# Two heads side by side in the TensorE array for the rough scores, one set of shift products, new engine orders and a stepped routing

## The chip, the cores and the metric

The kernel runs on one core of one Trainium2 chip. The metric is the device time of one execution in microseconds (us), the median of several runs. TensorE (PE) multiplies a loaded 128-column matrix with a moving one; VectorE (DVE), ScalarE (ACT) and GpSimd (POOL) work on 128 partitions; SyncE (SP) issues DMA transfers. Matrix products land in eight PSUM banks, everything else lives in SBUF.

## The reference

The input x is 8 sequences of 512 tokens with 128 features. The output is x plus attention times a gate:

```python
xn = _layernorm(x, axis=-1)
s = _L0_attn_ref(xn, W_qkv, W_out)        # 32 query heads of 64, 16 key/value heads, causal, ALiBi bias
g = _silu(_L0_ffn_ref(xn, gate_w, gate_b, w1, b1, w2, b2))   # 8 experts of width 512, top 2, softmax weights
x = x + s * g
```

Scores are q times k over sqrt(64), plus slope times (key position minus query position), with keys behind the query only; softmax; times v; all heads concatenated and projected. The feed-forward part picks two experts for each token and adds their weighted outputs.

## The kernel before, in words

Attention is cut into 64 bodies: one body is one sequence and one pair of key/value heads. A body has two slots (one key/value head each, `sl`), and a slot has two query heads (`h`). Every f32 value goes through TensorE as two f16 halves (hi and lo) in three products, to keep f32 precision.

The first 32 bodies (`HALF`) are followed by the expert part (blocks of 256 gathered token rows, loops over `hidden` and `down`), then come the other 32 bodies. During the first 32 bodies GpSimd also scatters the token rows to the slots of their experts (tasks `I` and `D`, two indirect DMAs for each 128 tokens), and the expert weights are split (`W`). During the second 32 GpSimd gathers the expert outputs (`I`, `D`, `G`).

The work of a body is cut into tasks with one letter and a number:

- `Q0`, `Q1`, `K0`, `V0`: projections of queries, keys, values (PE, then ACT takes the hi half and DVE the lo half; SP stacks copies of q and k into `q_st` and `k_st` by DMA).
- `M`, `B`: the rough scores. The f16 hi halves of q and k are multiplied (`M`, function `rough`, into the banks `M_ps[0]` for the first head and `M_ps[1]` for the second), and DVE takes each query row's maximum with the mask and bias (`B`, function `peaks`). A head has three rounds: one product of 512 columns, two of 128 and 384, one of 256. So a body has 12 `M` tasks and 12 `B` tasks. The array's rows are the 128 rows of `q_raw`, which hold both heads; `k_st` has two extra planes (2 and 3) in which the keys stand in one half and zeros in the other, so that one product sees one head only.
- `C`: the maxima become the shift that softmax subtracts. They stand in columns of `spread`; four products with the identity turn them into rows (PE, function `turn_shifts`, into `M_ps[0]`), and ACT copies a row for each head into `q_st` (function `shifts`). Two `C` tasks a body, one a slot.
- `S`, `E`, `L`, `P`: exact scores in ten groups a body (PE), exponentials (ACT), the lo half of the exponentials (POOL, `t_lo`), products with the values (PE, 12 products of 64 or 65 columns a group).
- `N`, `A`, `O0`: normalise (DVE), hi and lo of the output (ACT, DVE), a transposing DMA (SP), projection with W_out (PE) and accumulation (DVE).

The order of the tasks on each engine is a table, `ORDER`: for each half and engine a list of (task, body offset, place). `one_window` issues the list once for each window `w`, a task with offset `o` for body `w + o`. An engine works its list strictly in this order and waits at semaphores. `G_USERS` says which tasks share the two PSUM banks `G_ps`, and `bank_free` waits for the user before. `run_bodies` writes the first and last windows out and puts the rest in a loop of two windows. The top-2 routing (which slot each token goes to) is computed on DVE: `choose` in three steps among the first `B` tasks, and the rest in one piece between the entry windows and window 0. PE's rank products stand there too. Products of window 0 wait for `routed`, since the ranks lie in a PSUM bank that they need.

## Time and profile before

| what | value |
|---|---|
| median of 3 runs | 1255.06 us (1253.67 to 1255.94) |
| the profiled execution | 1253.06 us |
| its span, first to last instruction | 1251.1 us |
| busy share of PE, DVE, ACT, POOL | 92%, 80%, 75%, 70% |
| mean granted TensorE clock | 0.981 of full |

A share is busy time over the span. PE counts as busy while any product is in flight, and products overlap, so a busy PE can still have room between the starts of its products. A row of a timeline gives the start, the duration and the instruction, and in brackets the idle time before it and what ended it.

### The profile page before, as it was taken

What the parts mean: (1) busy time and instruction counts of PE and PEld (TensorE: products, weight loads), DVE (VectorE), ACT (ScalarE), POOL (GpSimd) and SP (SyncE); (2) the same over time, 40 slices, a digit from 0 to 9 for tenths busy, and PEclk for the clock granted to TensorE, in tenths of its full rate; (3) what the DMA queues carried; (4) which work ended last, traced back from release to release, by engine and by line L of the source; (5) the groups of instructions that cost most, each with busy time, mean ns of one, the idle gap of its engine ahead of it and who ended that gap; (6) DMA issues with size and microseconds to landing.
All of it is one profiled execution on the core that took longest, in us unless ns stands there. A gap on an engine that the chain in (4) does not pass through costs nothing. (4 is left out here: it accounts for less than half of the span.)

```text
span 1251.1 us, 52908 instructions
## 1 busy us (share of the span) xinstructions
PE 1154.0 (92%) x17226; PEld 912.5 (73%) x17226; DVE 1005.5 (80%) x3099; ACT 939.0 (75%) x1807; POOL 878.3 (70%) x1086
## 2 busy tenths in 40 slices
PE   2579999999999999987999779999999999999994
PEld 0357777777777777766888657777777777777873
DVE  8778888888888888764777648888888888888885
ACT  2468888888888888775666458888888888888884
POOL 9048888888888888875000058888888888888885
PEclk9989999999999999999999979999999999999997
DMA  8326666666666666644433456555555555555663
GB/s 243 158 57 144 143 147 151 143 143 144 144 144 144 144 143 143 147 107 86 87 90 86 94 129 141 136 135 134 134 134 134 134 134 134 134 134 134 138 139 95
DMA packets 286161, 165.28 MB, mean 132 GB/s; under 512 B 174994, under 2 KB 274674, under 8 KB 285428
## 3 DMA queue, kind: packets, MB, share of 16 engines
q1 hardware_dynamic: 281972, 155.63, 54.7%
q0 software_dynamic: 4096, 8.40, 2.3%
q8 instruction: 59, 0.97, 0.3%
q14 instruction: 34, 0.28, 0.1%
HBM read 15.76 MB, written 16.78 MB: 26 GB/s over the span
## 5 line engine op out<-in xcount | busy, mean ns | idle before, releaser
L781 POOL TENSOR_TENSOR t_lo<-stage 128x512 f16<-128x512 f32 x640 | 654.4, 1038 | 148.7 <-ACT stage L1180 144.5
L1392 DVE CUSTOM_DVE_ANT_0 stage<-ps,kmask 128x512 bf16<-128x512 f32 (+3 forms) x1024 | 466.2, 488 | 110.7 <-PE ps L878 91.9
L1180 ACT ACTIVATE stage<-ps,slope 128x512 f32<-128x512 f32 (+1 forms) x768 | 456.8, 620 | 126.8 <-PE ps L913 80.7
L904 PE MATMUL ps<-q_st,k_st 128*128 128x256 f16 (+3 forms) x1024 | 302.5, 301 | 4.0 <-DMA k_st<-stage 1.8
L936 PE MATMUL outs<-v_sp,stage 128*128 128x65 f16 x2560 | 283.3, 194 | 12.2 <-DVE stage L1422 9.0
L938 PE MATMUL outs<-v_sp,stage 128*128 128x64 f16 x2560 | 283.1, 194 | 0.0
L940 PE MATMUL outs<-v_sp,t_lo 128*128 128x65 f16 x2560 | 283.0, 194 | 0.0
L878 PE MATMUL ps<-k_st,stage 128*128 128x512 f16 (+3 forms) x1024 | 252.8, 304 | 14.9 <-DVE spread L1392 7.6
L936 PEld LDWEIGHTS outs<-v_sp,stage 128*128 128x128 bf16 x2560 | 239.4, 98 | 21.5 <-issue 11.2
L938 PEld LDWEIGHTS outs<-v_sp,stage 128*128 128x128 bf16 x2560 | 236.5, 98 | 8.9 <-issue 0.3
L940 PEld LDWEIGHTS outs<-v_sp,t_lo 128*128 128x128 f16 x2560 | 236.5, 98 | 0.0
L905 PE MATMUL ps<-q_st,k_st 128*128 128x128 f16 x1024 | 224.0, 219 | 0.0
L908 PE MATMUL ps<-q_st,k_st 67*128 67x384 f16 (+2 forms) x768 | 211.5, 275 | 0.0
L1169 ACT CAST q_st<-ps 1x512 f16<-1x512 f32 x256 | 147.9, 578 | 32.5 <-PE ps L887 27.2
L913 PE MATMUL ps<-late_q,late_k 66*128 66x134 f16 (+1 forms) x640 | 136.0, 212 | 0.0
L904 PEld LDWEIGHTS ps<-q_st,k_st 128*128 128x128 f16 x1024 | 100.4, 98 | 34.7 <-issue 14.3
L734 POOL COPY slot_now<-slot_of 128x1 uint32 (+1 forms) x128 | 23.2, 183 | 144.6 <-DMA slot_y<-stage 144.6
L878 PEld LDWEIGHTS ps<-k_st,stage 128*128 128x128 f16 x1024 | 84.3, 98 | 53.0 <-issue 24.3
L1125 ACT ACTIVATE stage<-ps,qscale 128x512 f16<-128x512 f32 x128 | 88.5, 691 | 44.9 <-PE ps L816 36.9
L905 PEld LDWEIGHTS ps<-q_st,k_st 128*128 128x128 f16 x1024 | 100.4, 98 | 17.2 <-issue 0.6
L908 PEld LDWEIGHTS ps<-q_st,k_st 67*128 67x128 f16 x768 | 74.8, 97 | 51.7 <-issue 1.9
L1422 DVE TENSOR_TENSOR stage<-outs,stage 128x512 f16<-128x512 f32 x128 | 88.0, 687 | 21.7 <-ACT stage L1160 21.7
(205 smaller groups left out, 2702.1 us busy)
## 6 DMA issues: line engine op xcount, KB each, us to landing
k_st<-stage SPq DMA_DIRECT2D x256, 128.0 KB, 2.4
q_st<-stage SPq DMA_DIRECT2D x256, 128.0 KB, 2.4
q_st<-stage SPq DMA_DIRECT2D x256, 64.0 KB, 2.1
k_st<-stage SPq DMA_DIRECT2D x128, 64.0 KB, 2.1
slot_y<-stage SPq DMA_DIRECT2D x40, 128.0 KB, 2.0
X<-in_L_attn_inputs SPq DMA_DIRECT2D x8, 512.0 KB, 8.0
slot_x<-att SPq DMA_DIRECT2D x2, 2048.0 KB, 8.7
wx_raw<-in_L_ffn_w SPq DMA_DIRECT2D x64, 64.0 KB
```

The source lines that it names most:

```text
L781: pool.tensor_tensor(t_lo[r], t_p[r], upper(t_p[r]), ALU.subtract).then_inc(s[f"lo{u % NG}"], 1)
L878: mm = pe.matmul(M_ps[h][:, c0:c0 + w], q_raw[sl][:, 0, i * P:(i + 1) * P], k_st[par][sl][:, 2 + h, 0:w], start=True, stop=True)
L904: pe.matmul(d, k[:, 0, at], q[:, 0, seen], start=(c0 == 0), stop=False, skip_group_check=True)
L905: pe.matmul(d[:, 0:P], k[:, 1, at], q[:, 1, at], start=False, stop=True, skip_group_check=True)
L908: pe.matmul(d[:, P:], k[far, 1, at], q[far, 1, (kt + 1) * P:SEQ], start=False, stop=True, skip_group_check=True)
L913: pe.matmul(d, late_k[late, :], late_q[late, LATE:P].unsqueeze(1).to_broadcast([P - LATE - 1, len(first), P - LATE]), start=False, stop=Tr ...
L936: pe.matmul(d, p_hi, v[:, with_one], start=(opens and i == kt), stop=False, skip_group_check=True)
L938: pe.matmul(d[:, OUT_COL[sl]:OUT_COL[sl] + DH], p_hi, v[:, lo], start=False, stop=False, skip_group_check=True)
L940: mm = pe.matmul(d, t_lo[r][:, c], v[:, with_one], start=False, stop=(closes and i == QT - 1), skip_group_check=True)
L1169: ins = act.copy(q_st[sl][h][DH:DH + 1, 1, :], M_ps[0][SHIFT[h]:SHIFT[h] + 1, :])
L1180: e = act.activation(t_p[r][:, c0:c1], S_ps[u % 2][:, c0:c1], ACT.Exp, scale=slope[:, bass.ds(pair_index(n) * 2 * SLOTS + sl * 2 + h, 1)])
L1392: ins = dve.tensor_tensor_reduce(junk[h][:, c0:c0 + w], M_ps[h][:, c0:c0 + w], kmask[:, SEQ - w:SEQ], -1.0 / 1024, 3e38, ALU.add, ALU.min, ...
```

## The change

1. Rough scores. `rough` now takes both heads of a round in one `M` task: for each piece of columns one product on the array's rows 0 to 63 (head 0, into `M_ps[0]`) and one on rows 64 to 127 (head 1, into `M_ps[1]`). Six `M` tasks a body in place of twelve; the number and width of the products stays. A round now waits for the peaks of both heads of the round before. The zero-padded planes of `k_st` are gone, and with them one of three DMAs of each key stacking and half of another.
2. Shifts. One `C0` on PE for both slots: the four head maxima stand in columns 0, 32, 64, 96 of one `spread` buffer (two buffers, by body parity), four products in place of eight, into a bank of `G_ps` and no longer into `M_ps[0]`. ACT still copies four rows.
3. All of `ORDER` and `G_USERS` are new.
4. Routing. The piece ahead of window 0 is cut into eight steps `route(0..7)`, put behind tasks of windows 0 to 2 of DVE (`FIRST_ONES`); PE's ranks stand behind a `V0`, and ACT copies them out of PSUM (`kept`). Scattering starts at body 4 in place of body 2; in bodies 7, 10, 13 and 16 two groups of 128 tokens are sent, with a third buffer.
5. Small: the first `V` task behind the `Q` tasks, the Exp table loaded earlier, windows 0 to 17 of the first half written out, ACT's last fill task of the second half ahead of the last expert output.

```diff
@@ rough scores and shifts on PE
-                sl, r, h = round_of(j)
+                sl, r = divmod(j, NR)
                 need(pe, f"qh{sl}", n + 1)
-                need(pe, f"kst{sl}", (n + 1) * 48)
-                if r > 0:
-                    need(pe, f"peak{sl}{h}", n * NR + r)
-                elif h == 0:
-                    need(pe, f"crow{1 - sl}", n + sl)
-                else:
-                    need(pe, f"peak{1 - sl}{h}", (n + sl) * NR)
+                need(pe, f"kst{sl}", (n + 1) * 32)
+                for h in range(2):
+                    if r > 0:
+                        need(pe, f"peak{sl}{h}", n * NR + r)
+                    else:
+                        need(pe, f"peak{1 - sl}{h}", (n + sl) * NR)
...
                 for i, c0 in ROUNDS[r]:
                     w = (i + 1) * P
-                    mm = pe.matmul(M_ps[h][:, c0:c0 + w], q_raw[sl][:, 0, i * P:(i + 1) * P],
-                                   k_st[par][sl][:, 2 + h, 0:w], start=True, stop=True)
-                mm.then_inc(s[f"rough{sl}{h}"], 1)
-
-            def turn_shifts(n, _, sl):
-
-                for h in range(2):
-                    need(pe, f"peak{sl}{h}", (n + 1) * NR)
-                for i in range(QT):
-                    mm = pe.matmul(M_ps[0][:, i * P:(i + 1) * P], spread[sl][:, i, :], ident16[:, :],
-                                   start=True, stop=True)
-                mm.then_inc(s[f"turnc{sl}"], 1)
+                    for h in range(2):
+                        head = slice(DH * h, DH * h + DH)
+                        mm = pe.matmul(M_ps[h][:, c0:c0 + w], q_raw[sl][head, 0, i * P:(i + 1) * P],
+                                       k_st[par][sl][head, 0, 0:w], start=True, stop=True)
+                mm.then_inc(s[f"rough{sl}"], 1)
+
+            def turn_shifts(n, par, _):
+
+                bank_free(n, "C0")
+                for sl in range(SLOTS):
+                    for h in range(2):
+                        need(pe, f"peak{sl}{h}", (n + 1) * NR)
+                for i in range(QT):
+                    mm = pe.matmul(bank_of("C0")[:, i * P:(i + 1) * P], spread[par][:, i, :], ident16[:, :],
+                                   start=True, stop=True)
+                mm.then_inc(s["turnc"], 1)
@@ key stacking on SP
-                sp.dma_start(to[DH:2 * DH, 0:4:3, :], hi.unsqueeze(1).to_broadcast([DH, 2, SEQ]))\
-                  .then_inc(s[f"kst{sl}"], 16)
-                sp.dma_start(to[0:DH, 2, :], hi).then_inc(s[f"kst{sl}"], 16)
+                sp.dma_start(to[DH:2 * DH, 0, :], hi).then_inc(s[f"kst{sl}"], 16)
@@ peaks on DVE
-                dve.wait_ge(s[f"rough{sl}{h}"], n * NR + r + 1)
+                dve.wait_ge(s[f"rough{sl}"], n * NR + r + 1)
@@ the sharing of the two G banks
-        [("V0", 1), ("O0", -2)],
-        [("Q1", 1), ("K0", 2), ("Q0", 2)],
+        [("Q1", 1), ("K0", 2), ("O0", -2)],
+        [("V0", 1), ("Q0", 2), ("C0", 1)],
@@ the first lines of PE's order of the first half
-            ("S0", 0, 0), ("M11", 0, 2), ("S1", 0, 3), ("P7", -1, 6), ("C1", 0, 9), ("P8", -1, 10), ("P9", -1, 13),
+            ("S0", 0, 0), ("M1", 1, 3), ("P9", -1, 5), ("S1", 0, 7), ("S2", 0, 11), ("Q1", 1, 14), ("M2", 1, 19),
@@ which groups of 128 tokens are sent with body n
+        FIRST_SENT, TWICE = 4, (7, 10, 13, 16)
-            return [t for t in range(NT) if min(t + UNROLL, HALF - UNROLL + (t - NT) // 2 + UNROLL) == n]
+            t = n - FIRST_SENT + len([b for b in TWICE if b <= n])
+            more = [(t - 1, UNROLL, TWICE.index(n))] if n in TWICE else []
+            return more + [(t, n % UNROLL, (n - FIRST_SENT) // UNROLL)]
@@ where the routing steps stand
-        CHOICE = {"B1": 0, "B3": 1, "B5": 2}
+        FIRST_ONES = {"DVE": [("B1", 0), ("B3", 0), ("B5", 0), ("B3", 1), ("B5", 1), ("N0", 0), ("B3", 2), ("B5", 2),
+                              ("N0", 1), ("B3", 3), ("B5", 3)],
+                      "PE": [("V0", 1)], "ACT": [("E4", 0)]}
```

Before the change, PE in its loop of the first half has the two heads' rounds of 256 columns (L878) apart, with a group of exact scores (L904 to L913) between them; L936 and L938 are products with the values.

```order
L878 MATMUL ps<-k_st,stage 128x256
L904 MATMUL ps<-q_st,k_st 128x512
L905 MATMUL ps<-q_st,k_st 128x128
L908 MATMUL ps<-q_st,k_st 128x384
L913 MATMUL ps<-late_q,late_k 128x67
L878 MATMUL ps<-k_st,stage 128x256
L936 MATMUL outs<-v_sp,stage 128x65
L938 MATMUL outs<-v_sp,stage 128x64
```

In the changed program the same round in the loop (L891 is `rough`, L825 to L827 are the three products of a projection) is:

```order
L825 MATMUL ps<-xT_hi,wq_hi 128x512
L826 REGISTER_ALU
L826 MATMUL ps<-xT_lo,wq_hi 128x512
L827 REGISTER_ALU
L827 MATMUL ps<-xT_hi,wq_lo 128x512
L301 REGISTER_ALU
L891 MATMUL ps<-k_st,stage 128x256 x2
```

The two heads' products now stand next to each other and nothing is between them; a round is between a query projection and a value projection.

On DVE before the change, the peaks (L1392) of two rounds follow each other with no other task between, here the loop's rounds of 128 and 384 columns of the second head and then the round of 256; L1400 is the lo half of the queries.

```order
L1392 ISA stage,spread<-ps,kmask 128x128
L1392 ISA spread 128x1
L1392 ISA stage,spread<-ps,kmask 128x384
L1392 ISA spread 128x1
L1385 REGISTER_ALU
L1392 ISA stage,spread<-ps,kmask 128x256
L1392 ISA spread 128x1
L1392 ISA stage,spread<-ps,kmask 128x256
L1392 ISA spread 128x1
L1400 ISA
```

In the changed program the normalisation (L1498, L1501) stands between these two rounds (L1462 is `peaks`, L1470 the lo half of the queries).

```order
L1462 ISA spread 128x1
L301 ISA
L1498 RECIPROCAL rden<-outs 128x8
L1501 TENSOR_TENSOR outs<-outs,rden 128x2x4x64
L1455 REGISTER_ALU
L1462 ISA stage,spread<-ps,kmask 128x256
L1462 ISA spread 128x1
L1462 ISA stage,spread<-ps,kmask 128x256
L1462 ISA spread 128x1
```

After the change each round's peaks are parted from the next round's by one or more other DVE tasks.

At the start, DVE of the changed program has the routing between tasks of windows 0 to 2. This is the place of `route(2)` in window 0 (L1419 to L1422), with the normalisation ahead of it and the peaks of a later round behind it:

```order
L1501 TENSOR_TENSOR outs<-outs,rden 128x2x4x64
L1419 TENSOR_TENSOR wx_lo<-per_e,ecmp 128x64
L1420 TENSOR_REDUCE per_e<-wx_lo 128x8
L1421 TENSOR_TENSOR per_e<-per_e 128x8
L1422 TENSOR_SCALAR per_e<-per_e 128x8
L1462 ISA stage,spread<-ps,kmask 128x256
L1462 ISA spread 128x1
```

Before, these four stood with 23 others in one run ahead of window 0 (L1478 to L1519), of which these are the first rows:

```order
L1478 TENSOR_SCALAR top<-top 128x32
L1479 RECIPROCAL top<-top 128x32
L1480 TENSOR_TENSOR top<-top 128x32
L1483 TENSOR_SCALAR ecmp<-ecmp 128x64
L1487 TENSOR_TENSOR wx_lo<-outs,wx_lo 128x128
L1489 TENSOR_REDUCE per_e<-wx_lo 128x8
```

The run is gone from between the peaks and window 0, and its rows are spread over three windows.

## Rows read from the trace of the kernel before

**Rows 1.** The page: busy shares, and tenths in 40 slices of 31.3 us.

```profile
PE 1154.0 (92%) x17226; PEld 912.5 (73%) x17226; DVE 1005.5 (80%) x3099; ACT 939.0 (75%) x1807; POOL 878.3 (70%) x1086
PE   2579999999999999987999779999999999999994
```

**Rows 2.** Windows, all engines: busy us of each, clock, DMA share, GB/s.

```profile
67.50:76.20 8.70, 0.07 (x2) 0.00 (x0) 8.05 (x25) 0.85 (x2) 2.04 (x2) 0.79 0.00 0
250.00:500.00 250.00, 248.54 (x3906) 198.48 (x3905) 216.95 (x693) 209.08 (x403) 216.81 (x259) 1.00 0.63 143
1000.00:1200.00 200.00, 199.75 (x3110) 158.24 (x3108) 170.75 (x550) 166.32 (x309) 163.41 (x194) 1.00 0.60 135
```

**Rows 3.** One instruction a body, in each half: durations ns, first and last start.

```profile
L1140 ACT ACTIVATE v_sp<-ps x25: 597/632/635, 127.9 to 500.6; 128x512 f16<-128x512 f32 x25
L1140 ACT ACTIVATE v_sp<-ps x25: 616/617/621, 809.8 to 1185.1; 128x512 f16<-128x512 f32 x25
```

**Rows 4.** Timeline of PE, first half: start us, duration us, instruction.

```profile
301.38 0.38 PE L887 MATMUL ps<-ident,spread 128*128 128x128 f16 x4
301.60 0.19 PE L936 MATMUL outs<-v_sp,stage 128*128 128x65 f16 x1
...
301.96 0.38 PE L814 MATMUL ps<-xT_hi,wk_hi 128*128 x1
...
302.61 0.27 PE L904 MATMUL ps<-q_st,k_st 128*128 128x256 f16 x1
302.72 0.22 PE L905 MATMUL ps<-q_st,k_st 128*128 128x128 f16 x1
...
303.60 0.59 PE L878 MATMUL ps<-k_st,stage 128*128 128x512 f16 x2
304.03 0.22 PE L814 MATMUL ps<-wo_hi,aT 128*128 x1
...
305.37 0.33 PE L904 MATMUL ps<-q_st,k_st 128*128 128x384 f16 x1
305.53 0.22 PE L905 MATMUL ps<-q_st,k_st 128*128 128x128 f16 x1
```

**Rows 5.** Groups by line and form, 250 to 500 us: busy us, mean ns, idle before.

```profile
L1392 DVE CUSTOM_DVE_ANT_0 stage<-ps,kmask 128x512 bf16<-128x512 f32 x66 | 42.8, 686 | 8.3 <-PE ps L878 8.3
L1392 DVE CUSTOM_DVE_ANT_0 stage<-ps,kmask 128x256 bf16<-128x256 f32 x64 | 27.2, 425 | 9.0 <-PE ps L878 4.0
L1407 DVE SCALAR_TENSOR_TENSOR stage<-ps,stage 128x512 f16<-128x512 f32 x16 | 11.1, 692 | 11.7 <-ACT stage L1133 11.7
L1180 ACT ACTIVATE stage<-ps,slope 128x512 f32<-128x512 f32 x129 | 88.8, 700 | 34.8 <-PE ps L913 34.8
L781 POOL TENSOR_TENSOR t_lo<-stage 128x512 f16<-128x512 f32 x162 | 166.5, 1036 | 27.9 <-ACT stage L1180 26.3
L758 POOL DMA_INDIRECT slot_x<-row_now,slot_now x32 | 31.9, 997 | 5.1 <-issue 5.1
L746 POOL TENSOR_TENSOR row_now<-mix,row_now 128x128 f16<-128x128 f16 x16 | 7.0, 436 | 0.5
L734 POOL COPY slot_now<-slot_of 128x1 uint32 x33 | 6.1, 185 | 0.0
```

**Rows 6.** Timeline of DVE and then PE at the start.

```profile
64.83 0.18 DVE L1478 TENSOR_SCALAR top<-top 128x32 f32<-128x32 f32 x1 [0.94 <-ACT top L1233]
...
75.14 0.23 DVE L1519 TENSOR_TENSOR slot_of<-slot_of,slot_bits 128x64 uint32<-128x64 uint32 x1
...
76.28 0.59 PE L887 MATMUL ps<-ident,spread 128*128 128x128 f16 x4 [8.71 <-DVE spread L1392]
```

**Rows 7.** Timeline of SP's queue, first half.

```profile
304.67 0.63 SPq L550 DMA_DIRECT2D k_st<-stage  x1
305.35 0.59 SPq L552 DMA_DIRECT2D k_st<-stage  x1
305.99 0.59 SPq L553 DMA_DIRECT2D k_st<-stage  x1
306.81 0.62 SPq L538 DMA_DIRECT2D q_st<-stage  x1
```

More of the change, by code:

```diff
@@ L289, in build @@
                 s[f"{step}{u}"] = sem(f"s_{step}{u}")
-        for step in ("rough", "peak"):
-            for j in ("00", "01", "10", "11"):
-                s[f"{step}{j}"] = sem(f"s_{step}{j}")
+        for sl in range(SLOTS):
+            s[f"rough{sl}"] = sem(f"s_rough{sl}")
+            for h in range(2):
+                s[f"peak{sl}{h}"] = sem(f"s_peak{sl}{h}")
         block = ctx.enter_context(nc.Block())
@@ L344, in run_bodies @@
         def run_bodies(eng, engine_name, tasks, lo, hi):
-            start, end = lo + 2 * UNROLL, hi - 2 * UNROLL
+            start, end = lo + (max(TWICE) + UNROLL if lo == 0 else 2 * UNROLL), hi - UNROLL
             for w in range(lo, start):
@@ L420, in weights_split, with over_e @@
             eng.wait_ge(s["wlo"], len(SPLITS))
+        L, t1, one1, L2, one2, cw = (lg[:, i, :, :] for i in range(6))
+        rank_of, total_of = L, t1[:, 0, :]
+        def over_e(a):
+            return a.unsqueeze(2).to_broadcast([P, NT, E])
+        ev = eidx[:, :].unsqueeze(1).to_broadcast([P, NT, E])
         RANK = E * FC
@@ L694, in _ @@
                     pool.memset(v_sp[par][:, :, col:col + 1], 1.0)
-            for sl in range(SLOTS):
-                pool.memset(spread[sl][:, :, :], 0.0)
+            for par in range(UNROLL):
+                pool.memset(spread[par][:, :, :], 0.0)
             for i in range(WORD):
@@ L1080, in _ @@
                         step_of(i_, c, g)
-            for j in ("00", "01", "10", "11"):
-                pe.wait_ge(s[f"peak{j}"], HALF * NR)
+            for sl in range(SLOTS):
+                for h in range(2):
+                    pe.wait_ge(s[f"peak{sl}{h}"], HALF * NR)
             for sl in range(SLOTS):
@@ L1288, in _ @@
                     outputs(j, c - 1)
+            begin_half("ACT", tasks, HALF, BODIES, fill_part(STEPS - 1, STEP - 1, 0))
             outputs(STEPS - 1, STEP - 1)
-            for g in range(PARTS):
+            for g in range(1, PARTS):
                 begin_half("ACT", tasks, HALF, BODIES, fill_part(STEPS - 1, STEP - 1, g))
@@ L1474, in _ @@
             dve.wait_ge(s["attz"], 1)
-            enter_bodies("DVE", {**tasks, "Y": lambda n, _, k: choose(k)}, 0, HALF)
-            dve.wait_ge(s["topexp"], 1)
-            small(dve.tensor_scalar(top[:, 6, :], top[:, 5, :], WS, WS, ALU.mult, ALU.add))
-            small(dve.reciprocal(top[:, 6, :], top[:, 6, :]))
-            small(dve.tensor_tensor(top[:, 7, :], top[:, 6, :], top[:, 5, :], ALU.mult))
-            blocks, first, end, first_slot = (per_e[:, i, :] for i in range(4))
-            small(dve.tensor_scalar(ecmp[:, :, :], ecmp[:, :, :], 0.0, None, ALU.is_gt))
@@ L1523, in _ @@
             dve.wait_ge(s["zeros"], 16 * ZERO_DMAS)
-            run_bodies(dve, "DVE", tasks, 0, HALF)
+            run_bodies(dve, "DVE", {**tasks, "Y": lambda k: route(k - CHOICES)}, 0, HALF)
             leave_bodies("DVE", tasks, 0, HALF, late=LATE_O)
```

218 lines of the change are left out of this document (117 added, 101 removed), and 48 rows, old and new, of the table ORDER.

## The prediction

> **What bounds the kernel now.** I read the page first. PE is busy 92% of the span, and in the tenths by slices it is at 9 but at the start, at two places in the middle (into the expert part and out of it) and at the end [rows 1]. So I cut out stretches of the two attention halves. From 250 to 500 us PE is busy 248.5 of 250 us, at full clock, DVE and POOL 217 and ACT 209; from 1000 to 1200 us PE has 199.75 of 200, DVE 171, ACT 166 and POOL 163 [rows 2]. TensorE is the bound, but a busy share can't say by how much, since products overlap. I take the time of a body from an instruction that runs once in each: 24 intervals from 127.9 to 500.6 us are 15.53 us a body, and 24 from 809.8 to 1185.1 are 15.64 [rows 3].
>
> For PE's real floor I use start to start. Four products of 128 columns take 0.22 us (301.38 to 301.60), so 0.056 each. Twelve with the values take 0.36, so 0.030 each. Three of 512 take 0.65 (301.96 to 302.61), so 0.216 each; 256 columns take 0.11 and 384 take 0.16 [rows 4]. A body has 120 value products (3.60 us), exact scores (a head takes 0.54 for L904's widths of 512, 384, 256 and 128, 0.33 for L908's 384, 256 and 128, 0.22 for four of L905, so four heads 4.36), ten late marks of 67 or 134 columns (0.48), rough scores 4 x (0.216 + 0.16 + 0.11 + 0.056) = 2.17, projections of queries, keys and values 1.30 + 0.65 + 0.67, output projection 24 x 0.056 = 1.34, shifts 8 x 0.056 = 0.45. The sum is 15.0 us. The kernel needs 15.53 and 15.64, so it runs 3.5 to 4% above the floor of its busiest engine. The waits agree: ACT sits 34.8 us of these 250 until PE's scores, POOL 27.9 until ACT, DVE 8.3 and 4.0 until PE's rough scores and 11.7 until ACT [rows 5].
>
> The floors of the others follow from the shares: DVE 216.95/250 x 15.53 = 13.5, POOL 13.5 and another 0.3 of issue time ahead of its two indirect DMAs (5.1 us for 32), ACT 13.0 [rows 2, 5]. In the second half, 13.35, 12.8 and 13.0.
>
> **The change, part by part.** *Rough scores.* The same 16 products of 2.17 us a body, but now in pairs on separate halves of the array's rows and into separate banks. No product of this trace uses 64 rows, so the price of a pair has to be bounded. If a pair runs one behind the other, it costs what it costs now: 0 saved. If the two stream together, half goes: 1.08 us a body. I take the second, since nothing in the two products is shared (rows, operands' partitions, bank) and issue is no obstacle: value products with their weight loads start every 0.030 us [rows 4], so the second of a pair of 512 could start 0.03 behind the first. With that lag a body's eight pairs give back 0.2, and I keep 0.9 to 1.1 saved.
>
> The trace has only one kind of array use, so what it costs to go from 128 rows to 64 and back is unknown too. From below it is nothing. From above it is a full drain: a product of 128 columns lasts 0.22 us where the next starts after 0.056, so 0.16 us [rows 4], 12 times a body (six rounds, in and out), 1.9 us. I take near nothing, because the nearest thing in the rows, the step from one kind of product to another (L887 to L936 at 301.60, L878 to L814 at 304.03), shows no gap at all; the drain is a rival below.
>
> The Trainium skill bears on both. Its page "TensorE: Matmul & The Clock Gate", Part 3, says that products on distinct row groups run at once with starts some 4 ns apart. By that page the pairs would save the whole 1.08. Its page "TensorEngine Tiling (Array Packing)", Key Properties, says that changing the tiling mode drains TensorE. By that rule there would be twelve drains a body and, at the price above, the rival's time below. No run so far shows either.
>
> *Shifts.* Four products fewer a body, 0.22 us of PE. ACT's four row copies stay. The old `turn_shifts` used `M_ps[0]`, so rough scores waited for ACT's copies; now they wait for the peaks alone.
>
> *Floor after.* 15.0 - 1.0 - 0.22 = 13.7 to 13.8 us on PE. That is level with POOL's 13.8 in the first half and close to DVE's 13.5. Nothing is taken off these two. So the body falls not by 1.3 but to the common floor and what four nearly full engines lose to each other. One full engine lost 3.5 to 4%; for three I take 5%: 13.75 x 1.05 = 14.45 us. The best I can argue is the old 3%, 14.2; the worst 15.0, where the gain of PE is half lost.
>
> *Order.* A round now waits for both heads' peaks, so the two banks no longer take turns. In the old order the peaks of one round followed those of the next at once; in the new one DVE always has another task of 0.5 to 1.4 us between, in which PE can refill both banks (the excerpts of the order show it). What queues behind a late round on PE is a projection or a value group, and behind late peaks on DVE the normalisation that ACT and the transposing DMA wait for. I cost it inside the 5%.
>
> *SP.* Each key stacking was three DMAs of 0.63 to 0.68 us on the queue (304.67 to 306.81 with the gap) [rows 7]; one goes, twice a body, 1.3 us of queue time. PE's steady stretch shows no wait of note for keys (its idle time is 1.5 of 250 us [rows 2]), so this is worth nothing by itself. The DMA engines are at 0.63 [rows 2].
>
> *Number of bodies.* The full-rate stretch of the first half is from about 88 to 540 us, 452/15.53 = 29 bodies; of the second from 740 to 1215, 475/15.64 = 30. The saving is 29 x 1.08 + 30 x 1.19 = 67 us.
>
> *Sending.* The first sends come two bodies later, and four bodies send twice: another two indirect DMAs (2 x 1.0 and 2 x 0.16), one subtraction (0.44) and two copies (0.37) on POOL, 3.1 us [rows 5]. Against 14.45 a POOL with 13.8 + 3.1 overruns by 2.4; buffers of exponentials take up part, and the old kernel doubled up in two bodies too. Net cost 4 us (0 to 8).
>
> *Routing.* DVE's run from 64.83 to 75.37 us holds PE up for 8.7 us [rows 6], and in 67.50 to 76.20 PE does nothing [rows 2]. Spread over windows 0 to 2 it adds 3.5 us to each; with no accumulation yet (0.69) DVE needs 13.5 - 0.7 + 3.5 = 16.3 there against 14.45, so 5.6 us come back. Net gain 3 us (0 to 8). The rest (tables loaded earlier, fill order, the transition to the second half) I put at 0, plus or minus 4.
>
> *Sum.* The profiled execution had 1253.06 us: 1253 - 67 + 4 - 3 = 1187. Runs have their median 2 us above it, 1255.06, so 1189.
>
> **The rivals.**
> - *The pairs don't overlap.* For: nothing in this trace shows that two products ever do more than pipeline. Then PE's floor is 15.0 - 0.22 = 14.8, times 1.035 is 15.3; 29 x 0.23 + 30 x 0.34 = 17 us less, with the +1 of the other parts 1239 us. The change would then not do what it says.
> - *A drain at each change of rows.* For: six rounds a body, each wedged between products on all rows. Against: no such gap between different products today. With 0.16 us, 12 times, PE's floor is 13.75 + 1.9 = 15.65, times 1.035 is 16.2: 29 x 0.67 + 30 x 0.56 = 36 us more, 1292 us: slower. It decides from (15.0 - 13.75)/12 = 0.10 us a switch on.
> - *The rounds in lockstep.* Both heads wait for each other. If each of six rounds makes DVE idle 0.25 us (it idled 0.13 for each of 64 rounds of 512 columns before [rows 5]), DVE's 13.5 becomes 15.0: 29 x 0.53 + 30 x 0.64 = 35 less, 1221 us. For: DVE is nearly full. Against: the tasks that the order puts between.
>
> **How the numbers follow.** Chances: the forecast 0.64 (own range 1174 to 1208, from 14.2 to 14.75 us a body), no overlap 0.13, drain 0.13, lockstep 0.10. A measurement of this kernel tells 0.2% (2.5 us) from no change. Faster are the forecast, lockstep, most of no overlap, and a drain below 0.1 us: 0.83. Same 0.03, slower 0.14. The range leaves out 1 in 10 or so above (a dear drain) and a little below: 1172 to 1245.
>
> **What the profile after would show.** The two products of a pair of 512 start within 0.05 us of each other, not 0.216, and the round lasts some 0.25 us from its start to the next product's. The once-a-body ACT instruction comes every 14.2 to 14.8 us. DVE and POOL are busy 93% or more of a steady stretch, and idle times on DVE shift from waiting for L878's successor to waits of all kinds. PE has no idle time of 8 us near 70 us. Four windows of the first half are longer by 1 to 2 us. I am wrong if pairs start 0.2 us apart, if a gap of 0.1 us or more stands ahead of or behind each round, or if bodies take over 15 us with PE's floor at 13.8.

## The result, and the profile after

The changed kernel takes 1240.49 us (median of 4 runs, 1236.63 to 1241.53) against 1254.37 us of the kernel before, measured beside it: ratio 0.9884, 95% interval 0.9861 to 0.9907. It is 1.2% faster where 5.2% was forecast (1189 us), still inside the stated range of 1172 to 1245. The profiled execution's span is 1238.8 us, 12.3 less than before.

The busy shares of the changed kernel, as in [rows 1], and the weight loads (PEld) of its rough products.

```profile
PE 1134.3 (92%) x16970; PEld 836.3 (68%) x16970; DVE 994.9 (80%) x3099; ACT 929.2 (75%) x1808; POOL 873.8 (71%) x1082
L891 PEld LDWEIGHTS ps<-k_st,stage 64*128 64x128 f16 x1024 | 40.1, 93 | 109.9 <-issue 95.1
```

PE stays at 92%. The second row is a first clue: the 1024 loads of 64 rows have 109.9 us of idle time ahead of them, 95.1 of it "issue", that is, a wait for nothing the profile can name. Some of that is normal: the same loads on all rows have 53.1 us of it (the run e1 below, `issue: 53.1, 111`). The 42 us on top are about 0.11 for each of the 384 visits (64 bodies of six rounds).

Windows of the changed kernel, columns as in [rows 2]:

```profile
75.00:100.00 25.00, 19.37 (x262) 13.40 (x262) 19.41 (x62) 14.14 (x27) 11.32 (x12) 0.86 0.37 74
100.00:125.00 25.00, 20.96 (x299) 15.02 (x297) 20.77 (x69) 17.43 (x35) 15.14 (x15) 0.93 0.46 94
250.00:500.00 250.00, 246.30 (x3846) 178.49 (x3844) 212.24 (x689) 207.97 (x404) 220.27 (x268) 1.00 0.58 129
```

In the steady stretch PE is still busy 246.3 of 250 us. DVE is at 85% (87% before) and POOL at 88% (87% before). So four nearly full engines, which the forecast had, never came about. The third number from the end is the granted TensorE clock: 0.86 and 0.93 in the first two stretches, so a part of each ran at the lower of the clock's two levels, 1.2 in place of 2.4 GHz. The two missing shares add up to at most 5 us (0.14 x 25 + 0.07 x 25, an estimate).

The instruction that runs once a body, as in [rows 3]; the first row is the first windows, the second the steady part of the first half, the third that of the second half:

```profile
L1158 ACT ACTIVATE v_sp<-ps x5: 597/597/599, 132.6 to 193.0; 128x512 f16<-128x512 f32 x5
L1158 ACT ACTIVATE v_sp<-ps x16: 596/597/600, 258.2 to 491.9; 128x512 f16<-128x512 f32 x16
L1158 ACT ACTIVATE v_sp<-ps x26: 610/612/622, 796.5 to 1181.2; 128x512 f16<-128x512 f32 x26
```

That is 15.10, 15.58 and 15.39 us a body, against 15.53 and 15.64 before; forecast was 14.45.

The timeline of PE in the first half, to be read against [rows 4]:

```profile
302.26 0.38 PE L827 MATMUL ps<-xT_hi,wq_lo 128*128 128x512 f16 x1
302.57 0.28 PE L891 MATMUL ps<-k_st,stage 64*128 64x256 f16 x2
302.78 0.23 PE L825 MATMUL ps<-wv_hi,xT_hi 128*128 128x128 f16 x1
...
304.38 0.22 PE L928 MATMUL ps<-late_q,late_k 66*128 66x134 f16 x1
304.54 0.39 PE L891 MATMUL ps<-k_st,stage 64*128 64x512 f16 x2
304.86 0.39 PE L825 MATMUL ps<-xT_hi,wk_hi 128*128 128x512 f16 x1
...
305.30 0.38 PE L827 MATMUL ps<-xT_hi,wk_lo 128*128 128x512 f16 x1
```

The pair overlaps as forecast: two products of 512 columns are one row of 0.39 us, 0.01 longer than one alone (L827), where two on all rows took 0.59 [rows 4]. But a gap stands on either side. The product at 304.38 has 134 columns, worth 0.06, so the pair could start at 304.44 and starts at 304.54: 0.10. A product of 512 needs 0.216 until the next start, which would be 304.76; L825 starts at 304.86: 0.10 again. From 304.44 to 304.86 is 0.42 to 0.43 us, exactly what the two products took on full rows (303.60 to 304.03 in [rows 4]). For 256 columns it is worse: from 302.48 (302.26 plus 0.216) to 302.78 is 0.30, where two on full rows need 0.22. A gap of 0.1 us on either side of each round was one of the prediction's own signs of being wrong.

The weight loads around the same pair change their place too:

```profile
304.53 0.10 PEld L891 LDWEIGHTS ps<-k_st,stage 64*128 64x128 f16 x2
304.85 0.10 PEld L825 LDWEIGHTS ps<-xT_hi,wk_hi 128*128 128x128 f16 x1 [0.23 <-issue]
305.09 0.10 PEld L827 LDWEIGHTS ps<-xT_hi,wk_lo 128*128 128x128 f16 x1
```

L827's load (305.09) runs beneath the product before it and is 0.21 us ahead of its own (305.30). L891's and L825's loads are not pulled ahead: each begins 0.01 us before its product. So at a change between 64 and 128 rows no load runs ahead. Whether the 0.10 us are the load itself, which lasts as long, or the array running empty, these rows can't tell.

**Where 12.3 us of span came from.** The same instruction, before and after, between like bodies:

```profile
L1140 ACT ACTIVATE v_sp<-ps x4: 597/598/634, 81.6 to 127.9; 128x512 f16<-128x512 f32 x4
L1140 ACT ACTIVATE v_sp<-ps x26: 597/632/635, 127.9 to 515.9; 128x512 f16<-128x512 f32 x26
L1140 ACT ACTIVATE v_sp<-ps x3: 628/630/632, 515.9 to 555.8; 128x512 f16<-128x512 f32 x3
L1140 ACT ACTIVATE v_sp<-ps x30: 606/617/621, 762.8 to 1215.8; 128x512 f16<-128x512 f32 x30
```

```profile
L1158 ACT ACTIVATE v_sp<-ps x4: 597/603/629, 73.9 to 132.6; 128x512 f16<-128x512 f32 x4
L1158 ACT ACTIVATE v_sp<-ps x26: 590/597/600, 132.6 to 522.7; 128x512 f16<-128x512 f32 x26
L1158 ACT ACTIVATE v_sp<-ps x3: 597/597/597, 522.7 to 553.1; 128x512 f16<-128x512 f32 x3
L1158 ACT ACTIVATE v_sp<-ps x30: 610/612/622, 751.4 to 1196.5; 128x512 f16<-128x512 f32 x30
```

The start got worse: the first body is 7.7 us earlier (73.9 against 81.6, the routing run is gone), but three windows then take 58.7 us in place of 46.3, so window 3 begins 4.7 us later. The next 25 bodies take 390.1 us in place of 388.0, and 8 us of that are the doubled sends: without them (the run e9 below, `132.1 to 514.4`) the same 25 take 382.3, 0.23 less a body than before. The last two of the half take 30.4 us in place of 39.9, 9.5 saved. There the kernel before had its own doubled sends (bodies 30 and 31), and its PE stood for 6.2 us behind DVE (`PE outs L936 <- DVE stage L1422: 6.2, 2, 4.2`), DVE behind ACT (`DVE stage L1422 <- ACT stage L1160: 7.3, 2, 4.8`), and ACT behind the DMA of a send (`ACT row_now L1204 <- DMA slot_x<-row_now,slot_now: 7.6, 3, 4.2`). In the second half 29 bodies take 445.1 us in place of 453.0, 0.27 less each. The rest, 1.7 us, lies in the expert part and the ends.

So a steady body became 0.23 to 0.27 us shorter. The prediction's price for the four shift products that are gone is 0.22 us a body. That fits, but no run here takes the shifts out, so what shortens the steady bodies is not shown; the third key DMA, below, is another candidate for a part.

### The profile page after: what moved, and what is told of

Same layout as the page of the kernel before. It is cut to its first block and busy times, and to the rows that moved or that the text cites. A ratio compares the mean times of both kernels' runs of the same rounds, so it can differ in the third digit from the quotient of the medians.

```text
span 1238.8 us, 51239 instructions
## 1 busy us (share of the span) xinstructions
PE 1134.3 (92%) x16970; PEld 836.3 (68%) x16970; DVE 994.9 (80%) x3099; ACT 929.2 (75%) x1808; POOL 873.8 (71%) x1082
## 5 line engine op out<-in xcount | busy, mean ns | idle before, releaser
L1462 DVE CUSTOM_DVE_ANT_0 stage<-ps,kmask 128x512 bf16<-128x512 f32 (+3 forms) x1024 | 451.5, 488 | 109.4 <-PE ps L891 84.3
L1198 ACT ACTIVATE stage<-ps,slope 128x512 f32<-128x512 f32 (+1 forms) x768 | 440.7, 618 | 96.5 <-PE ps L928 83.9
L951 PE MATMUL outs<-v_sp,stage 128*128 128x65 f16 x2560 | 263.4, 195 | 6.8 <-POOL t_lo L792 5.9
L953 PE MATMUL outs<-v_sp,stage 128*128 128x64 f16 x2560 | 262.3, 194 | 0.0
L955 PE MATMUL outs<-v_sp,t_lo 128*128 128x65 f16 x2560 | 262.2, 194 | 0.0
L891 PE MATMUL ps<-k_st,stage 64*128 64x512 f16 (+3 forms) x1024 | 139.0, 309 | 25.0 <-DVE spread L1462 23.5
L747 POOL COPY slot_now<-slot_of 128x1 uint32 (+1 forms) x128 | 23.1, 183 | 153.2 <-DMA slot_y<-stage 153.2
L891 PEld LDWEIGHTS ps<-k_st,stage 64*128 64x128 f16 x1024 | 40.1, 93 | 109.9 <-issue 95.1
L1281 ACT ACTIVATE X<-ps,b1T 128x256 f32<-128x256 f32 x160 | 67.1, 472 | 57.1 <-PE ps L827 57.1
```

Source lines behind the costliest of these rows:

```text
L891: mm = pe.matmul(M_ps[h][:, c0:c0 + w], q_raw[sl][head, 0, i * P:(i + 1) * P], k_st[par][sl][head, 0, 0:w], start=True, stop=True)
L951: pe.matmul(d, p_hi, v[:, with_one], start=(opens and i == kt), stop=False, skip_group_check=True)
L953: pe.matmul(d[:, OUT_COL[sl]:OUT_COL[sl] + DH], p_hi, v[:, lo], start=False, stop=False, skip_group_check=True)
L955: mm = pe.matmul(d, t_lo[r][:, c], v[:, with_one], start=False, stop=(closes and i == QT - 1), skip_group_check=True)
L1198: e = act.activation(t_p[r][:, c0:c1], S_ps[u % 2][:, c0:c1], ACT.Exp, scale=slope[:, bass.ds(pair_index(n) * 2 * SLOTS + sl * 2 + h, 1)])
L1462: ins = dve.tensor_tensor_reduce(junk[h][:, c0:c0 + w], M_ps[h][:, c0:c0 + w], kmask[:, SEQ - w:SEQ], -1.0 / 1024, 3e38, ALU.add, ALU.min, ...
```

## The experiments

Edits are against the changed kernel unless said; ratios are to the kernel before, measured beside each run. "After" below is the changed kernel's 0.9884 [0.9861, 0.9907].

**Pairs against full rows: e1_full_rows and e2_half_columns.** In e1 each rough product runs on all 128 rows, so it adds both heads' scores, and the slopes are 0 to keep exponentials small. TensorE streams what it did before the change, with no change of rows. e2 is e1 with half the columns of each rough product (half of the rough scores are left out): the streaming time of the pairs without their switches.

```diff
-                        mm = pe.matmul(M_ps[h][:, c0:c0 + w], q_raw[sl][head, 0, i * P:(i + 1) * P],
-                                       k_st[par][sl][head, 0, 0:w], start=True, stop=True)
+                        mm = pe.matmul(M_ps[h][:, c0:c0 + w], q_raw[sl][:, 0, i * P:(i + 1) * P],
+                                       k_st[par][sl][:, 0, 0:w], start=True, stop=True)
```

> The changed kernel with one thing undone: each rough product runs on all 128 rows of the array again (it then adds up both heads, so the shifts are wrong; all ALiBi slopes are set to 0 so that exponentials stay finite; nothing of that changes the amount of work). Theory A, a switch between 128 and 64 rows costs 0.1 us each and eats what the pairs save: 12 x 0.1 = 1.2 us of switches go and 8 x 0.135 = 1.08 us of streaming come back, so the time stays within 5 us of the changed kernel's 1240. Rival B, the pairs save 1.08 us a body and something else bounds the body at 15.4 us: PE then has 1.08 us more a body, and the time rises by 20 to 60 us.

> As the run before (all 128 rows, slopes 0), but each rough product has only half its columns, so half of the rough scores is left out: PE streams exactly what the pairs stream, and there is no switch of rows. Theory A: the body falls to what I forecast for the changed kernel, 14.3 to 14.7 us, and the time to 1185 to 1205. Rival B (DVE, POOL, ACT or the waits between them hold the body at 15.4 us, whatever PE does): 1230 to 1245.

e1: 0.9867 [0.9843, 0.9891], no slower than the pairs. e2: 0.9539 [0.9519, 0.9559]. The once-a-body instruction of e1 (first windows, second half):

```profile
L1157 ACT ACTIVATE v_sp<-ps x4: 597/597/597, 136.7 to 181.5; 128x512 f16<-128x512 f32 x4
L1157 ACT ACTIVATE v_sp<-ps x26: 586/605/622, 802.9 to 1187.1; 128x512 f16<-128x512 f32 x26
```

and of e2 (first windows, steady first half, second half):

```profile
L1157 ACT ACTIVATE v_sp<-ps x4: 599/640/643, 135.0 to 177.9; 128x512 f16<-128x512 f32 x4
L1157 ACT ACTIVATE v_sp<-ps x17: 597/640/643, 254.1 to 493.1; 128x512 f16<-128x512 f32 x17
L1157 ACT ACTIVATE v_sp<-ps x27: 584/620/631, 765.1 to 1146.7; 128x512 f16<-128x512 f32 x27
```

e1 needs 14.93 and 15.37 us a body, the pairs 15.10 and 15.39: on the whole, side by side in the array saves TensorE nothing. e2 needs 14.30, 14.94 and 14.68, where 14.45 was forecast. So the other engines would have allowed most of the forecast: e2's ratio is 0.0345 below the changed kernel's, 43 us of 1254. That is what the switches cost this kernel. On TensorE alone they are 71 us (12 x 0.10 in 59 bodies); without them the bodies run into other waits, so not all of it comes back.

**The price of a switch by itself: e3_micro, e5_micro_lines.** Both are a short run of products on data in SBUF and compute nothing of the reference. In e3 one line issued everything and the trace merged the rows, so it could not tell the kinds apart; e5 gives each kind a line of its own.

> PE alone on constants, nothing waits: runs of twelve products of 512 columns on 128 rows, on rows 0 to 63 only, on rows 0 to 63 and 64 to 127 in turn into separate banks, then rounds of six 128-column products on 128 rows followed by a pair on halves of 512 or of 128 columns, the same pair on all 128 rows, and on 67 rows. Theory A: halves in turn start 0.11 us apart on average (two in 0.216), and each pair on halves among products on 128 rows has some 0.1 us of gap ahead of it and behind it, 0.2 a round, whatever its width; 67 rows show no gap. Rival B: no gap beyond 0.02 us without the kernel's waits.

> The isolated TensorE test again, each kind of product on a line of its own so that the trace keeps them apart. After the first test, theory A: twelve products of 512 columns take 2.59 us on 128 rows and on 64 rows of one half, and 1.3 us on halves in turn; a pair of 512 among 128-row products takes 0.32 us from its start to the next product's start and starts 0.1 us late (0.43 together, as two products on 128 rows take, so a round of 512 gains nothing), a pair of 128 costs 0.27 together against 0.11 on 128 rows, so it loses 0.15; with 67 rows there is no gap. Rival: gaps of 0.1 us only in the full kernel.

e5 on PE. L47 is twelve full-row products of 512 columns as a mark, L55 twelve in turn on the upper and lower half, L51 twelve on rows 0 to 63 alone, L59 six full-row products of 128, L63 a pair on halves, L67 two on full rows, L75 two pairs in one visit. The granted clock is 1.00. A period below is the time from one visit's start to the next one's.

```profile
9.64 2.76 PE L51 MATMUL outs<-b,a 64*128 64x512 f16 x12
12.34 2.76 PE L47 MATMUL outs<-b,a 128*128 128x512 f16 x12
15.03 1.47 PE L55 MATMUL outs<-b,a 64*128 64x512 f16 x12
16.43 2.76 PE L47 MATMUL outs<-b,a 128*128 128x512 f16 x12
...
19.57 2.76 PE L47 MATMUL outs<-b,a 128*128 128x512 f16 x12
22.17 0.50 PE L59 MATMUL outs<-b,a 128*128 128x128 f16 x6
22.60 0.39 PE L63 MATMUL outs<-b,a 64*128 64x512 f16 x2
22.93 0.51 PE L59 MATMUL outs<-b,a 128*128 128x128 f16 x6
23.36 0.39 PE L63 MATMUL outs<-b,a 64*128 64x512 f16 x2
...
32.04 0.23 PE L63 MATMUL outs<-b,a 64*128 64x128 f16 x2
...
32.65 0.23 PE L63 MATMUL outs<-b,a 64*128 64x128 f16 x2
...
36.01 0.50 PE L59 MATMUL outs<-b,a 128*128 128x128 f16 x6
36.35 0.59 PE L67 MATMUL outs<-b,a 128*128 128x512 f16 x2
...
37.11 0.59 PE L67 MATMUL outs<-b,a 128*128 128x512 f16 x2
...
41.24 0.28 PE L67 MATMUL outs<-b,a 128*128 128x128 f16 x2
...
41.68 0.28 PE L67 MATMUL outs<-b,a 128*128 128x128 f16 x2
...
54.10 0.60 PE L75 MATMUL outs<-b,a 64*128 64x512 f16 x4
...
55.08 0.60 PE L75 MATMUL outs<-b,a 64*128 64x512 f16 x4
```

Halves in turn: twelve take 1.40 us (15.03 to 16.43). Twelve on full rows take 2.69 when a run on halves follows (12.34 to 15.03) and 2.60 when full rows follow (19.57 to 22.17), so a change of rows at the end is 0.09 to 0.10 of each, and halves in turn do run two at a time: 1.30 against 2.60. Twelve on one half alone take as long as full rows (9.64 to 12.34, 2.70): only the turns between the halves save. With full-row products between, one period with a pair of 512 is 0.76 us (22.60 to 23.36) and with two on full rows 0.76 (36.35 to 37.11): even, with no wait for anything. Ahead of the pair six products of 128 take 0.43 to the next start (22.17 to 22.60), ahead of a full-row product 0.34 (36.01 to 36.35): 0.09 for the switch in. Behind it the pair lasts 0.33 (22.60 to 22.93) where one product's stream is 0.216: 0.11 for the switch out. The cost doesn't depend on the width: a period with a pair of 128 is 0.61 (32.04 to 32.65), where one with two full-row products of 128 is 0.44 (41.24 to 41.68). With two pairs of 512 in one visit a period is 0.98 (54.10 to 55.08), where four on full rows would give 1.20 (0.34 + 4 x 0.216), so it pays to stay.

**The old order: e4_old_order_pairs and e12_old_order_both_heads.** The kernel before, with both heads' rounds issued in the second head's task: on halves in e4, on all rows against the zero-padded planes in e12. The pairing of the heads is in both, and with it the first head's products move to the place of the second head's task, in an order that was not made for it; the switches are in e4 alone.

```diff
+                if h == 0:
+                    return
...
+                for h in range(2):
+                    if r > 0:
+                        need(pe, f"peak{sl}{h}", n * NR + r)
+                    else:
+                        need(pe, f"peak{1 - sl}{h}", (n + sl) * NR)
```

> The kernel before, with its own orders, routing, key stacking and shifts, but the second head's rough task of each round issues both heads' products as pairs on halves of the rows, and the first head's task issues nothing. Theory A: PE's floor changes by -1.08 + 1.2, so the body is 15.5 to 15.9 us and the time 1250 to 1275 (a little worse than before, since a round also waits for both heads' peaks). Rival B (pairs save and the new order loses): the time falls to 1200 to 1225.

> The kernel before, with both heads' products of a round in one task (of the second head, as in the run with the old order and pairs, which took 1.074 of before) but each on all 128 rows against the zero-padded planes, so there is no change of rows. It tells lockstep from switches in that run. Theory: lockstep is all of it, since a switch with pair costs as much as full rows on the whole (0.2 us a body more): ratio 1.06 to 1.075. Rival: the switches cost a good part there: ratio 1.00 to 1.04.

e4: 1.0737 [1.0719, 1.0754], a miss: neither of my two ranges had it. e12: 1.0691 [1.0674, 1.0707]. The peaks on DVE in 250 to 500 us, e4 and then e12:

```profile
L1398 DVE CUSTOM_DVE_ANT_0 stage<-ps,kmask 128x512 bf16<-128x512 f32 (+1 forms) x238 | 105.0, 488 | 40.8 <-PE ps L883 40.8
```

```profile
L1398 DVE CUSTOM_DVE_ANT_0 stage<-ps,kmask 128x512 bf16<-128x512 f32 (+1 forms) x240 | 105.7, 487 | 43.1 <-PE ps L883 43.1
```

DVE waits 41 and 43 us for PE's rounds in both; the changed kernel's peaks wait 23.1 for them in the same window, and two widths of the old kernel's 8.3 and 4.0 [rows 5]. So in the old order pairing the heads costs 0.069 of 1254, 87 us, and pairs on halves with their switches are 6 us dearer than full rows. In the new order full rows in lockstep (e1) take 0.9867. So the new lists make the pairing of the heads bearable; the overlap adds no gain in TensorE's time. These two runs do not show that the lists gain something by themselves.

**The key stacking: e6_full_rows_correct, e13_third_dma, e14_wide_dma, e15_old_order_two_dmas.** e6 has rough products on full rows as the kernel before computes them: zero-padded planes, cleared at the start, the second DMA of a stacking writing two planes, and the third DMA. e13 and e14 keep the pairs and add the third DMA, or the second plane of the second one, to planes that nothing reads. e15 is the kernel before with two DMAs (its rough products add both heads; slopes 0).

```diff
@@ e6 and e13
+                sp.dma_start(to[0:DH, 2, :], hi).then_inc(s[f"kst{sl}"], 16)
@@ e6 and e14
-                sp.dma_start(to[DH:2 * DH, 0, :], hi).then_inc(s[f"kst{sl}"], 16)
+                sp.dma_start(to[DH:2 * DH, 0:4:3, :], hi.unsqueeze(1).to_broadcast([DH, 2, SEQ]))\
+                  .then_inc(s[f"kst{sl}"], 16)
```

> The changed kernel with the rough scores computed as before: zero-padded key planes, the third key DMA, products on all 128 rows; new orders, shifts, sends and routing stay. Theory A (switches eat what pairs save): same time as the changed kernel, 1236 to 1246 us, unless SP's queue with 1.3 us more a body becomes late. Rival B: 1270 or more.

> The changed kernel (pairs on 64 rows) plus the third DMA of each key stacking, into a plane that nothing reads, and every wait for the stacking waits for it too. Theory (queue time and completion of that DMA cost the new order its gain): 6 to 12 us above the changed kernel's 0.988, ratio 0.993 to 0.998. Rival (it is the full-row products together with the planes, not the DMA): ratio 0.987 to 0.990.

> The changed kernel with the second DMA of each key stacking writing two planes in place of one (twice the bytes, the same number of DMAs), the second read by nothing. If bytes cost (DMA share 0.58 in its first half against 0.63 before), 3 to 6 us: ratio 0.991 to 0.993. If only the count on the queue does, ratio 0.987 to 0.990.

> The kernel before with the two-DMA key stacking of the changed one; the rough products stay on 128 rows and read both heads' keys (so the shifts are of the sum of two heads, and the slopes are 0 to keep the exponentials small). The prediction gave the third DMA nothing, since TensorE was not waiting for keys in the old order: ratio 0.998 to 1.002. If it costs there too what it does in the new order: 0.990 to 0.993.

e6: 1.0006 [0.9990, 1.0023], a miss; I had expected it near e1. e13: 0.9922 [0.9900, 0.9944], between my two ranges. e14: 0.9886 [0.9853, 0.9920], the rival's. e15: 0.9969 [0.9950, 0.9988], between my two ranges again. The estimates put the third DMA at 0.4% (5 us) in the new order and 0.3% (4 us) in the old one, and its bytes at nothing. The interval of e13 touches the changed kernel's, so the 5 us are likely, not certain; e15's alone excludes nothing saved. e6 is another 0.8% above e13. The once-a-body instruction first runs at 77.0 us in e6 and at 73.3 in e13, which is 3.7 us (clearing planes on GpSimd stands there). The two profiled spans are 1255.0 and 1250.5 us, 4.5 apart, so in these traces the start is most of it; what would make up the 10 us by the ratios I did not find. e6 also says what the pairs are good for. e1 adds both heads and so is no substitute; with full rows and the heads apart, as in e6, nothing is left of the gain (1.0006 against 0.9884, 15 us). Pairs save no time in the array on balance, but they let the planes and the DMA go.

**The sends: e9_28_sends.** The doubled sends of bodies 7, 10, 13 and 16 are taken out, so 4 of 32 groups of token rows are not scattered and their part of the output is missing.

```diff
-            t = n - FIRST_SENT + len([b for b in TWICE if b <= n])
-            more = [(t - 1, UNROLL, TWICE.index(n))] if n in TWICE else []
-            return more + [(t, n % UNROLL, (n - FIRST_SENT) // UNROLL)]
+            return [(n - FIRST_SENT, n % UNROLL, (n - FIRST_SENT) // UNROLL)]
```

> The changed kernel with 28 of its 32 groups of 128 token rows scattered: the second sends of bodies 7, 10, 13 and 16 are gone (the four last groups are not sent, so their part of the output is missing). The four bodies that send twice took 16.4, 18.5, 17.0 and 16.5 us in the changed kernel, where their neighbours take 15.1, so by my account of the places the doubled sends cost 1.3 + 3.4 + 1.9 + 1.4 = 8 us plus 1 to 3 in the bodies behind. Theory (sends cost it): ratio to the kernel before 0.980 to 0.982, 8 to 10 us below the changed kernel's 0.988. Rival (those bodies are long because the written-out part meets the loop or PE has it anyway, as no neighbouring row proves the sends): ratio 0.986 to 0.989.

0.9833 [0.9818, 0.9848]: 6.4 us below the changed kernel, less than the 8 to 10 I expected. The ten bodies that hold all four doubled sends take 159.0 us in the changed kernel (first row) and 151.0 in e9 (second row), 15.10 each as in the windows ahead of them.

```profile
L1158 ACT ACTIVATE v_sp<-ps x11: 590/597/600, 193.0 to 352.0; 128x512 f16<-128x512 f32 x11
```

```profile
L1155 ACT ACTIVATE v_sp<-ps x11: 589/597/598, 192.5 to 343.5; 128x512 f16<-128x512 f32 x11
```

**The loop and the routing: e7_written_out, e8_one_run, e10_split_written_out, e11_best.** e7 writes all windows out in place of the loop of two. e8 puts all eight routing steps behind the normalisation of window 0. e10 is e7 with each doubled send's second DMA put into the next window. e11 is e10 and e8 together.

```diff
-            with eng.Fori(start // UNROLL, end // UNROLL) as i_:
-                for c in range(UNROLL):
-                    one_window(engine_name, tasks, i_ * UNROLL + c, lo, hi, c)
+            for w in range(lo, hi):
+                one_window(engine_name, tasks, w, lo, hi, w)
@@ e8
-        FIRST_ONES = {"DVE": [("B1", 0), ("B3", 0), ("B5", 0), ("B3", 1), ("B5", 1), ("N0", 0), ("B3", 2), ("B5", 2),
-                              ("N0", 1), ("B3", 3), ("B5", 3)],
+        FIRST_ONES = {"DVE": [("B1", 0), ("B3", 0), ("B5", 0), ("N0", 0)],
```

> The changed kernel with all windows of both halves written out in place of loops of two windows. Bodies come every 15.10 us in its written-out windows and alternate 15.70 and 15.10 (mean 15.40) in the loops. If the loop is what costs 0.3 us a body, 44 bodies give 13 us: 1225 to 1230 us. Rival: the 0.3 comes from elsewhere (the sends, instruction fetch), and the time stays at 1240 or rises.

> The changed kernel with the eight routing steps in one run of 10.5 us on DVE behind the first normalisation of window 0, in place of steps over windows 0 to 2. Those windows take 19.5 us each in the changed kernel against 15.1 later, 13 us for the three. If DVE's 10.5 us are simply added because DVE has no room, the time stays within 3 us. If cutting the run up costs more than the run (each step delays a product that PE waits for), it falls by 3 us or more. If one run leaves PE idle for longer, it rises by 3 us or more.

> All windows written out (1230.7 us alone, 0.982), and of each doubled send the second DMA of its first group is moved into the next window. If the doubled sends hold GpSimd up because two pairs of indirect DMAs stand in one window, the spread gives back half of 8 us: ratio 0.977 to 0.980. If it is only the total work of GpSimd that counts, the long bodies become two less long ones and the ratio stays at 0.981 to 0.983.

> Windows written out, doubled sends spread over two windows, routing in one run ahead of window 0 with its first normalisation, pairs on 64 rows. The three were worth 8, 0 to 4 and 4.6 us apart; if they add up, 1254 times 0.988 less 12.6 to 16.6: 1223 to 1227 us, ratio 0.975 to 0.978. If the one run and the written-out windows save the same waits, 0.980 to 0.982.

e7: 0.9822 [0.9798, 0.9846], 8 us below the changed kernel, where 13 were expected. e8: 0.9847 [0.9828, 0.9866], 4.6 us below by the estimates, with intervals that overlap. e10: 0.9768 [0.9745, 0.9792], 6.8 us below e7, where 4 were expected. e11: 0.9733 [0.9717, 0.9749], 1221.69 us: the fastest here, 2.7% under the kernel before and 1.5% under the changed one. The once-a-body instruction in the second half of e7, and in e11's first and second half:

```profile
L1150 ACT ACTIVATE v_sp<-ps x26: 586/613/619, 804.1 to 1183.3; 128x512 f16<-128x512 f32 x26
```

```profile
L1161 ACT ACTIVATE v_sp<-ps x28: 589/597/599, 128.6 to 539.6; 128x512 f16<-128x512 f32 x28
L1161 ACT ACTIVATE v_sp<-ps x30: 587/614/621, 739.7 to 1178.5; 128x512 f16<-128x512 f32 x30
```

e7 needs 15.17 us a body where the loop needed 15.39; e11 needs 15.22 and 15.13. In e11 window 3 begins at 128.6, 4.0 us earlier than in the changed kernel (132.6). What in the loop costs 0.2 us a body I didn't take apart.

The routing's place, read from PE's waits between window 0 and window 3 of the changed kernel (73.9 to 132.6 us):

```profile
PE ps L825 <- DVE stage L1470: 5.6, 3, 3.4
PE ps L902 <- DVE stage L1470: 5.2, 2, 3.1
```

L1470 is the lo half of the queries on DVE. When it is done, a bank that keys (L825) or shifts (L902) wait for is free, and it stands behind the peaks and the routing steps in DVE's list. That is 10.8 us, and for peaks PE waits only 0.7 us more. With all steps in one run (e8) the same kind of wait is 11.2 us in the same windows (`PE ps L901 <- DVE stage L1469: 11.2, 2, 10.7`). So eight steps hid nothing: PE waited as long as with one run. The kernel before has 1.3 us of waits in these windows (81.6 to 127.9), at full granted clock, behind its one wait of 8.7.

## Why the prediction was right and wrong

**What bounds the kernel: right.** PE is the bound before and after, and its floor by start to start holds: e1's is 14.8 (the predicted 15.0 less the shifts), and its bodies between 136.7 and 181.5 us take 14.93.

**The pairs overlap: right.** Two at a time in the kernel and in e5 (1.30 against 2.60 us for twelve, without the change of rows at the end). The Trainium skill's page "TensorE: Matmul & The Clock Gate", Part 3, says that products on distinct row groups run at once, and here the runs agree. The rival of no overlap falls, though its time (1239) is the nearest: the right number by another cause. That the change is faster was forecast rightly, but the pairs, the reason given for most of the 67 us, give nothing on balance in the array; so the sign was luck in part.

**Nothing for a change of rows: this step failed.** The prediction took "near nothing" for the step from 128 rows to 64 and back, because steps from one kind of product to another show no gap [rows 4]. But those rows are all between products of over 64 rows, and so say nothing of a change. It costs 0.10 us, each way, twelve times a body: 1.2 us, where the pairs give 1.08. Put into the prediction's own sum, the floor is 13.75 + 1.2 = 14.95, and times 1.035 the body is 15.47, so the whole comes to 29 x 0.06 + 30 x 0.17 = 7 us saved less the 1 us of the other parts' sum, 1249 us, 9 above the measured 1240. The Trainium skill's page "TensorEngine Tiling (Array Packing)", Key Properties, says that changing the tiling mode drains TensorE. The runs agree that each change costs something, 0.10 us; whether the array drains in it they don't show. My rival priced it by a whole product's latency, 0.16, which is too dear and gave 1292; its break-even of 0.10 a switch is where the kernel landed.

**Body = floor x 1.05: about right.** e2, with the floor that was meant (13.75), needs 14.30, 14.94 and 14.68 us, that is 1.04, 1.09 and 1.07. The factor was a little low; the floor was the fault.

**Lockstep inside the 5%: right for the new order, and only there.** e1 has it and shows 14.93 and 15.37 on a floor of 14.8. In the old order pairing the heads costs 87 us (e12). The reason given, other DVE tasks between two rounds' peaks, fits: DVE waits 43 us of 250 for rounds in one order and 23 in the other, where it waited 12 before the change. But the two orders differ in every list, so that it is these tasks is argued and not shown.

**SP's third DMA at nothing: too low.** 4 us in the old order (e15), perhaps 5 in the new. "No wait of note for keys" was a loose reading: the 1.5 us that PE idled between 250 and 500 us are all waits for that stacking (`PE ps L904 <- DMA k_st<-stage: 1.5, 8`). From 740 to 1215 us they are 0.4, so the 4 us are not all in these waits, and by what path the DMA costs the rest is open.

**Sending 4 us (0 to 8): too dear, on balance.** The doubled sends cost the changed kernel 6.4 us (e9) to 8 (its ten bodies). But the kernel before paid for its own at the end of the half: its last two bodies take 9.5 us longer than the changed kernel's. So the new places cost about nothing net; the prediction named the old doubling and did not price it.

**Routing a gain of 3 us: wrong sign.** The first body came earlier, but the next three windows took 19.6 us on average, and window 3 begins 4.7 us later than before (by the trace of one execution, switches included). One run in window 0 (e8) is about 4.6 us better than eight steps. The prediction had counted DVE's total work. The trace shows what it left out: PE waits 10.8 us for the lo half of the queries, which stands behind the routing on DVE, and behind these waits the granted clock falls (0.86 and 0.93 in the first two stretches of 25 us).

**Shifts, 0.22 us a body of PE: not tested.** Steady bodies are 0.23 to 0.27 us shorter, which fits.

**The loop: not foreseen.** It costs the changed kernel 8 us (e7). The kernel before has such a loop too, and its 3.5 to 4% above the floor were read with it, so I don't count it in the miss. No run tells what it costs there.

Together: e2, with the streaming time that was meant and no switches, takes 0.9539 of before, 1197 us, 8 above the forecast. So the switches are 43 of the 51 us by which the forecast missed. The other 8 are what is left of the rest: the factor and the routing took more than was forecast, the DMA and the sends less. No run parts these 8 us.

## What to carry to other kernels

Two half-height products in the array at once save one product's stream and cost two switches, 0.20 to 0.21 us here: below some 500 columns a visit (counted for one of the two products) it doesn't pay, and several pairs in one visit do. When an operand shape appears in no row, equal steps between other shapes are no evidence that it is free; a short kernel with each kind on a line of its own, between marks of known length, settles the price. Before work is spread over several places of a strictly ordered engine, look at what stands behind each place: here the next task frees a bank, and TensorE waited 11.5 us for eight steps and 11.2 for one run.

## What the runs showed of the hardware

In these traces a weight load is pulled ahead beneath the product before it (305.09 for 305.30), but not over a change between 64 and 128 rows, in either direction. Products of 66 and 67 rows behave as full ones: no gap stands between them and products of 128 rows, in the kernel (66 and 67) or in e5 (67 only; here L71 is two of 67 rows and 128 columns, with a period of 0.45 us, as with 128 rows).

```profile
50.07 0.28 PE L71 MATMUL outs<-b,a 67*128 67x128 f16 x2
...
50.52 0.28 PE L71 MATMUL outs<-b,a 67*128 67x128 f16 x2
```

The gap belongs to the change and not to a wait on data: e5 has no semaphore between its products and shows 0.09 ahead of a pair and 0.11 behind it.
